# The first feed-forward block issued between the half images of a window attention, and one slot more ahead of the transposed probabilities

## What is computed

```python
def _L0_conv_ref(x, ...):                    # x: 16 x 16 x 16 x 96
    h = _layernorm(x, ln1_w, ln1_b)
    hw = ...                                 # 64 windows of 64 tokens
    qkv = hw @ qkv_w + qkv_b                 # 12 heads of 8
    attn = einsum('bhnd,bhmd->bhnm', q, k) * scale + bias
    attn = softmax(attn)
    out = einsum('bhnm,bhmd->bhnd', attn, v) ... @ proj_w + proj_b
    x = shortcut + h
    m = _layernorm(x, ln2_w, ln2_b)
    m = gelu(m @ mlp_w1 + mlp_b1) @ mlp_w2 + mlp_b2    # 96 -> 384 -> 96
    return x + m
```

## Time and profile before

| | before |
|---|---|
| median of 3 runs | 1312.55 us (1305.82 to 1316.09) |
| the profiled execution | 1309.46 us, of which span 1307.7 us |
| PE busy | 1154.8 us (88%), 8859 instructions |
| DVE busy | 740.0 us (57%) |
| ACT busy | 515.9 us (39%) |
| POOL busy | 387.1 us (30%) |
| mean granted clock of PE | 0.942 |

### The profile page before, as it was taken

One profiled execution on the slowest core, in us unless ns is written; L12 is line 12 of the kernel. 1 busy time (PEld: TensorE's weight loads), 2 busy tenths in 40 slices (PEclk: granted clock), 3 DMA queues, 4 the chain that ended last, 5 costly groups with the idle time before them and its releaser, 6 DMA issues. The chain is left out here.

```text
span 1307.7 us, 23695 instructions
## 1 busy us (share of the span) xinstructions
PE 1154.8 (88%) x8859; PEld 790.6 (60%) x8859; DVE 740.0 (57%) x2112; ACT 515.9 (39%) x839; POOL 387.1 (30%) x584
## 2 busy tenths in 40 slices
PE   4888879789887979999999997788888978999998
PEld 2565656566665656766666674466455544577776
DVE  3788844477772436666666666276455565333322
ACT  1555533343431333333343332345343422455543
POOL 3645445443425421010101210424100000353522
PEclk8999969899997989999999998699799999999999
DMA  4500000000000000000000000000000000000000
GB/s 88 100 11 2 2 2 0 1 1 1 2 1 1 0 1 1 1 1 1 1 1 1 1 2 1 1 1 1 1 2 1 2 2 1 2 13 7 9 11 13
DMA packets 28924, 9.39 MB, mean 7 GB/s; under 512 B 26961, under 2 KB 28816, under 8 KB 28816
## 3 DMA queue, kind: packets, MB, share of 16 engines
q1 hardware_dynamic: 25760, 7.02, 2.6%
q10 hardware_dynamic: 3056, 0.92, 0.3%
HBM read 6.36 MB, written 1.57 MB: 6 GB/s over the span
## 5 line engine op out<-in xcount | busy, mean ns | idle before, releaser
L156 POOL TENSOR_TENSOR ln_v<-MV,eps 128x2 f32<-128x2 f32 (+3 forms) x81 | 16.2, 201 | 427.2 <-PE bank L1132 247.3
L1194 ACT ACTIVATE fa_e<-bank 128x1024 f32<-128x1024 f32 x64 | 65.5, 1024 | 161.1 <-PE bank L1102 161.1
L1997 PEld LDWEIGHTS bank<-e_w,ex_G 128*128 128x128 f32 x768 | 90.6, 192 | 14.4 <-issue 14.1
L2112 DVE SCALAR_TENSOR_TENSOR X<-bank,ex_L,X 128x96 f32<-128x96 f32 x128 | 31.8, 311 | 114.0 <-PE bank L1997 108.1
L1246 DVE TENSOR_REDUCE fa_z<-bank 128x4 f32<-128x1024 f32 x64 | 78.3, 1223 | 26.3 <-PE bank L1084 24.7
L1989 PE MATMUL bank<-hT,e_w 96*128 96x512 f32 x192 | 90.6, 609 | 0.0
L1997 PE MATMUL bank<-e_w,ex_G 128*128 128x96 f32 x768 | 90.0, 274 | 0.0
L2040 ACT ACTIVATE ex_G<-bank,e_b 128x512 f32<-128x512 f32 x96 | 64.3, 686 | 61.7 <-PE bank L1989 58.9
L1844 DVE TENSOR_REDUCE ca_z<-bank 128x2 f32<-128x256 f32 x96 | 48.9, 552 | 49.3 <-PE bank L1571 49.2
L1102 PE MATMUL bank<-fa_a,fa_b 64*128 64x256 f32 x512 | 74.1, 409 | 1.1 <-DVE fa_a L1253 1.1
L1115 PE MATMUL bank<-fa_e,fa_v 128*64 128x256 f32 x512 | 72.0, 404 | 1.1 <-ACT fa_e L1194 1.1
(11 more groups left out here) (252 smaller groups left out, 2641.7 us busy)
## 6 DMA issues: line engine op xcount, KB each, us to landing
out_tokens<-X SPq DMA_DIRECT2D x8, 192.0 KB, 2.1
...
```

What stands on the lines that cost most here:

```text
L1194: act.activation(E[v % 2][:], k.banks[:, b:b + 2, :].rearrange("p i (c q) -> p i c q", c=2), ACT.Exp).then_inc(s["exp"], 1)
L1997: last = pe.matmul(bank[4 + e % 2][:, t * C:(t + 1) * C], G[e % 2][:, j, t * P:(t + 1) * P], k.ew2[:, e, j, :], start=(j == 0), stop=(j == ...
```

## The change

`mlp_in_pieces` is a new function. It issues the first feed-forward block in pieces, and `window_attention` calls for these pieces in its slots; the block is no longer a stage of its own. A step of the feed-forward block takes four slots, called r = 0 to 3 here, from slot 13 (`BEHIND`) to slot 44 (`LAST`), which is 13 slots after the last scores. All that the block puts into accumulator memory (transposes, three `up` products, `down`) goes through bank 6 alone, one after the other. So each `up` waits for the gelu of the one before. The two halves of the transposed probabilities share bank 2 now, and each waits until ACT has copied the other out. Probabilities are transposed in the third slot after their scores (before: the second), and what follows them is a slot later too. DVE spreads the keys of an image in the even slot in which ACT and PE want its queries and values; before it was in an odd slot, one and a half slots earlier. The extra product `keep_warm` is issued in 13 slots ahead of the scores and in 9 ahead of `attend`. Statistics of a norm are written to `k.MV` at once, without a copy (L195 and L408), save in the second feed-forward block, which is a loop with a register.

```diff
-def statistics(dve, k, s, n, count):
+def statistics(dve, k, s, n, count, first=0, unrolled=True):
...
+    if unrolled:
+        for t in range(count):
+            last = dve.bn_aggr(k.MV[:, n * count + t, :], k.stats[:, first + t, :])
+        last.then_inc(s["mv"], 1)
+        return
...
+def mlp_in_pieces(k, bank, ctx, prefix, w, prev):
...
+    def tensor(pe):
+        for m in range(steps):
+            pe.wait_ge(s["y"], 2 * m + 2)
+            after(pe, s["x"], m)
+            for t in range(4):
+                last = pe.transpose(bank[0:C, t * P:(t + 1) * P], k.Y[m % 2][:, 4 + t, :], k.ident[:])
+            last.then_inc(s["T"], 1)
+            yield
+            pe.wait_ge(s["hT"], m + 1)
+            for j in range(KH):
+                if j:
+                    pe.wait_ge(s["gelu"], KH * m + j)
+                pe.matmul(bank[:], w["w1"][:, j * P:(j + 1) * P], k.hT[m % 2][:], start=True, stop=True).then_inc(s["up"], 1)
+                yield
+            pe.wait_ge(s["gelu"], KH * (m + 1))
+            for t in range(4):
+                for j in range(KH):
+                    last = pe.matmul(bank[:, t * C:(t + 1) * C], G[:, j, t * P:(t + 1) * P], w["w2"][:, j, :], start=(j == 0), stop=(j == KH - 1))
+                if t == 1:
+                    yield
+            last.then_inc(s["down"], 1)
+            yield
...
     def probs_t
-                    after(pe, s["pte"], 2 * u - 1 + b)
+                    after(pe, s["pte"], 2 * u + b)
...
             def _(pe):
+                behind = later.tensor(pe)
                 for u in range(FIRST, LAST + 1):
                     n, odd = u // 2, u % 2 == 1
+                    r = (u - BEHIND) % 4 if u >= BEHIND else None
+                    if u == BEHIND:
+                        pe.wait_ge(s["late"], 16 * len(k.late))
                     if 0 <= u < HALVES:
                         scores(u)
...
+                    if 0 <= u - 3 < HALVES:
+                        probs_t(u - 3, 0)
+                    if r is not None:
+                        next(behind)
+                    if 0 <= u - 3 < HALVES:
+                        probs_t(u - 3, 1)
+                    if odd and 0 <= n - 3 < IMAGES:
+                        outputs_t(n - 3)
                     if odd and n + 2 < IMAGES:
                         queries_keys(n + 2)
...
+                    if 0 <= u - 4 < HALVES:
+                        attend(u - 4)
+                    if r == 1:
+                        next(behind)
                     if not odd and n + 2 < IMAGES:
                         tokens_t(n + 2)
...
+                    if r == 1:
+                        next(behind)
+                    if odd and 0 <= n - 3 < IMAGES:
+                        project(n - 3)
                     elif not odd and 0 <= n + 1 < IMAGES:
                         values(n + 1)
...
             def _(act):
...
+                    if odd and 0 <= n + 1 < IMAGES:
+                        values(n + 1)
+                    if 0 <= u - 3 < HALVES:
+                        pt_out(u - 3, 0)
+                    if 0 <= u - 1 < HALVES and r != 1:
                         exps(u - 1)
+                    if r == 1:
+                        next(behind)
+                    if 0 <= u - 3 < HALVES:
+                        pt_out(u - 3, 1)
...
             def _(dve):
...
+                    if 0 <= u - 5 < HALVES:
+                        heads_out(u - 5)
                     if 0 <= u < HALVES:
                         biased_scores(u)
...
+                    if not odd and 0 <= n - 4 < IMAGES:
+                        residual(n - 4)
+                    if not odd and 0 <= n + 1 < IMAGES:
+                        keys_by_head(n + 1)
+                    if r == 0 or r == 3 or (r == 1 and u > BEHIND + 1):
+                        next(behind)
```

144 lines of the change are left out of this document (91 added, 53 removed).

## The result

| | before | after |
|---|---|---|
| median | 1309.18 us (1304.63 to 1316.09, 4 runs) | 1347.01 us (1337.38 to 1358.63, 4 runs) |
| the profiled execution | 1309.46 us, span 1307.7 us | 1356.52 us, span 1354.7 us |
| PE busy | 1154.8 us (88%) | 1196.2 us (88%) |
| DVE busy | 740.0 us (57%) | 719.4 us (53%) |
| ACT busy | 515.9 us (39%) | 529.0 us (39%) |

A forecast was written before the change was run, and what follows sets the result against it. DVE was taken to bound the attention, PE the feed-forward block. 1309.5 + 4.9 (later convolution stage) + 10.8 (clock) - 2.7 (elsewhere) gave 1322.5 us; range 1300 to 1339, the forecast's own 1310 to 1332.

The forecast's parts named there:

- The chain of slots 0 to 12, +10: Attention slots 0 to 12: values wait for keys and queries, slots of 5.9 and 5.1, 66.8 us instead of 56.8.
- I take two more falls, 3.2: In the slots before the last two steps: new pauses make the clock fall twice, at 1.6 us each.
- 0.1 for the slow clock at the start: Start of slots 0 to 12: the slow clock adds 0.1 us to their 66.8.
- Slots 13 to 31, 113: Joined slots: r = 0 to 3 take 4.6, 7.8, 6.3 and 5.6; 113 us in all, slot 32 at 210.7.
- The tail, 41.5 and 7.6 for the clock: Slots 32 to 44 take 41.5 us, with steps near 10.7; low clock in the last two steps adds 7.6.
- Elsewhere, -2.7: Later stages: the dropped copies of 0.17 save 2.7 us in the convolution stage, where PE waits for DVE's statistics.
- The copies don't help: Slots 0 to 12: copies taken from DVE gain nothing, since DVE is no longer the bound.
- The clock falls in most steps: Rival for the joined and plain even slots: ten falls at 1.6 instead of two, 13 us more, 1335; chance 0.25.
- The table switch costs more: Rival for slots 14 to 34: eleven switches each hold ACT one load longer, 14 us more, 1337; chance 0.05.
- It gets faster: Rival for plain and joined slots: the waits fall into one another and two falls go, giving 1294; chance 0.15.
- the two clock terms: Clock falls: 7.6 us in the last two steps and 3.2 in the slots before, 10.8 together.

The follow-up runs named there:

- e2_fill: The changed kernel with four products on constants ahead of the waiting values in even slots 0 to 12: 1330.74 us, 1.019 of the kernel before.
- e12_filltail: The changed kernel with keys spread in the odd slot, plus three extra products behind each `up` of the last two steps: 1304.60 us, 0.996 of the kernel before.
- e10_copy: The changed kernel with keys spread in the odd slot and the statistics copies put back, except in `image_stats`: 1326.95 us, 1.016 of the kernel before.
- e1_keys: The changed kernel with DVE spreading the keys at the end of the odd slot again: 1308.27 us, 1.001 of the kernel before.
- e4_nocopy: The kernel before with statistics written to MV at once, without the copy, save in blocks run through `mlp`: 1281.76 us, 0.981 of the kernel before.
- e7_notable: The changed kernel with keys in the odd slot and the first block's gelu replaced by Identity, so no table switches: 1303.78 us, 0.997 of the kernel before.
- e5_keys_banks: The changed kernel with keys in the odd slot and the last three steps' `up` products in banks 3, 4 and 5: 1294.64 us, 0.990 of the kernel before.
- e8_split: The changed kernel with keys in the odd slot and the first feed-forward block a stage of its own again: 1309.10 us, 1.001 of the kernel before.

## Why the prediction was wrong, point by point

**The chain of slots 0 to 12, +10.** The durations were right: 5.99 and 5.21 at the full clock for 5.9 and 5.1, with the values waiting for the queries (0.99 <-ACT wa_q) and 0.67 of wait for the shared bank where 0.7 was said. But only slots 8 and 9 of the changed kernel ran so. Slot 13 started at 119.00 instead of 97.7, 21.3 later. That is where the prediction failed. Its step was "I take two more falls, 3.2", with a price of 1.6 for a fall, from one slot of the kernel before. Both factors were wrong: the low clock stayed for 23 us at a time (59 to 82), so that a fall cost four slots, about 8 us (slots 4 to 7 took 30.45 where two periods are 22.4), and there was another stay from 99 to 123. e2_fill shows that the clock is the cause and nothing else of that order: 15.6 of the 21.3 go with the pause filled, and the chain as long as before. The other 5.7 are mostly a second term that was mis-sized, the "0.1 for the slow clock at the start": slots 0 to 4 take 29.95 in e2_fill (29.84 to 59.79), where the sum has 22.7 for them at the full clock, and the granted clock is 0.50 there in 36 to 40 and 46 to 54. Slots 5 to 12, at the full clock, take 43.62 for 44.0.

**Slots 13 to 31, 113.** Right in kind and nearly in size: r = 0, 1, 2, 3 at the full clock 4.77, 7.96, 6.26, 5.78 for 4.6, 7.8, 6.3, 5.6. From slot 13 to slot 31 106.7 was worked out (204.4 less 97.7). At the full clock it is 109.7: e2_fill's 111.86 less the 2.2 by which its slots 26 and 27 stretch. It was 113.4 in the profiled execution. Here 3.0 were missed by small change in each slot, and 3.7 by the clock.

**The tail, 41.5 and 7.6 for the clock.** At the full clock 48.3 from slot 31 on in e12_filltail for 47.8. The clock fell in both steps, as the prediction had it, but the term for it was mis-sized. It took 0.87 for each of five `up` and 1.5 for each `down`; a `down` took 5.44 for 2.92, 2.5 more, and slot 31, one of the two sets of transposes (1.06 for 0.61) and the attention's last pieces were at the low clock too. The stretch took 64.5: 16.7 instead of 7.6.

**Elsewhere, -2.7.** The convolution stage took 157.45 for 160.22, -2.77, and in all other profiles without these copies 156.72 to 157.59; in e10_copy with copies 160.77. This term was right in size; its reason, that PE waits for each of them there, was not looked at. Of the later stages the third and the last shift by up to 7 us from profile to profile (353.0 to 359.7 in the kernels without copies, 356.1 in e10_copy and 362.3 before; 477.6 to 483.9 with and without them); that they cancel in this profile is luck.

**The sum.** 21.3 + 6.7 + 16.7 are 44.7 where 10.8 was allowed. The difference, 33.9, is that of the convolution stage (296.90 for 263.0), and nearly that of the profiled execution (1356.52 for 1322.5). Of the 44.7, some 3 are durations (3.0 in slots 13 to 31, 0.5 in the tail, 0.4 less in slots 5 to 12), and the rest, some 41, is the clock.

**"The copies don't help", and DVE.** Right for the plain slots of the order with the keys moved (e10_copy has the same lengths as e1_keys), wrong for the whole even there (18.7 us), and silent about what mattered more: in the order of before they are worth some 28 us (e4_nocopy). The change gave up that order, and with it the gain.

**The rivals.** *The clock falls in most steps* was the true one, had 0.25, and was priced at 13 more (1335); it was 34. The argument against it, that most pauses of that length had not made the clock fall before, was taken from an order in which DVE and not the chain made the pauses. *The table switch costs more* was wrong (e7_notable). *It gets faster* was placed 23 us below the sum, and the changed kernel is no such form. e5_keys_banks shows that a form with the chain and the tail mended is 1.0% faster than the kernel before, but it needs those two edits, and e8_split says that the joining is not what gives it. The page "TensorE: Matmul & The Clock Gate" of the Trainium skill, section "Why this matters for your kernels", names a gap longer than any pause from slot 4 on. By it the result would have been 1311.7, and the trace disagrees: from there to the convolution stage PE never waited for another engine for more than 1.11, and some 34 of the 41 us of the low clock lie in slot 5 and behind it. In slots 0 and 2 PE paused for 3.22 and 3.42, and of those two the trace does not tell.

**Direction and range.** Slower was the likeliest of the two signs (0.39 against 0.14), but within 1% had the most. The range ended at 1339, and the changed kernel's fastest executions are at 1337.4. It was too narrow because the forecast's own range took the two clock terms at twice their value at most.

Still open is what decides, from one execution to the next, whether the clock holds in slots 26 to 31; the three traces show that it differs, and not why.
